# Down projection of an eight-core transformer layer: every second weight-tile load issued from GpSimd instead of SyncE

## What is computed

```python
def ternary_quant(w):
    scale = jnp.mean(jnp.abs(w)) + EPS
    q = jnp.clip(jnp.round(w / scale), -1.0, 1.0) * scale
    return w + jax.lax.stop_gradient(q - w)
...
x = x + attention(layernorm(x))             # [2048, 2048] on each core
h = layernorm(x)
up   = einsum('bsd,ed->bse', h, wu)         # 8192 expert columns
gate = einsum('bsd,ed->bse', h, wg)
hidden = silu(up) * gate
return x + einsum('bse,de->bsd', hidden, wd)    # the down projection
```

## Time and profile before

| What | Value |
|---|---|
| five runs, us | 8733.61, 9023.23, 9047.79, 9153.85, 9173.29 (median 9047.79) |
| the profiled execution, us | 8739.01 |
| its span on the slowest core (core 2), us | 8737.3 |
| spans of the eight cores, us | 8699.1 to 8737.3 |
| granted TensorE clock, mean over the span | 0.746 to 0.751 |
| PE busy | 4945.0 us, 57% of the span |
| down projection: first matmul to end of the span | 7272.3 to 8737.3 us |
| tile loads `td` from SP | 512, 128 KB each |

### The profile page before, as it was taken

One profiled execution on the slowest core, in us unless ns is written; L12 is line 12 of the kernel. 1 busy time (PEld: TensorE's weight loads), 2 busy tenths in 40 slices (PEclk: granted clock), 3 DMA queues, 4 the chain that ended last, 5 costly groups with the idle time before them and its releaser, 6 DMA issues.

```text
span 8737.3 us, 69328 instructions; the slowest of 8 cores (8699.1 to 8737.3 us)
## 1 busy us (share of the span) xinstructions
PE 4945.0 (57%) x22987; PEld 2188.1 (25%) x22987; DVE 3214.0 (37%) x4854; ACT 1724.8 (20%) x3014; POOL 638.7 (7%) x1086
## 2 busy tenths in 40 slices
PE   1534444444444434366211199999999995666775
PEld 1111111111111111122111144444444442222222
DVE  4044424433433334221566555555555540000000
ACT  3133323323322323111111111211212110000000
POOL 0111111111111111000000000000000000000000
PEclk9755565556565665677555599999999998898998
DMA  2322222222222222422344322212112113223222
GB/s 80 33 78 84 80 50 80 80 68 62 73 73 65 72 68 86 93 82 73 106 130 132 124 81 76 81 74 82 75 75 80 75 54 124 77 85 117 70 69 78
DMA packets 316026, 709.36 MB, mean 81 GB/s; under 512 B 123584, under 2 KB 189152, under 8 KB 283552
## 3 DMA queue, kind: packets, MB, share of 16 engines
q0 software_dynamic: 157216, 350.46, 14.5%
q1 hardware_dynamic: 158464, 354.47, 12.3%
HBM read 607.32 MB, written 109.05 MB: 82 GB/s over the span
## 4 chain that ended last, share of the span: by engine, by line
PE 48%; DMA 18%; DVE 13%; ACT 9%; issue 7%; POOL 2%; another core or an unknown queue 1%; SPq 1%; DVEq 0%; ACTq 0%; POOLq 0%
PE up_ps L1222 11%; PE gt_ps L1236 10%; DMA td<-tdT_scr 7%; DMA tdT_scr<-tds 5%; PE a_ps L461 5%; PE po_a L1319 3%; PE pr_ps L863 3%; PE y_ps L736 3%; PE pt_ps L616 3%; PE po_b L1319 3%; DVE stt L654 2%; ACT slabA L1152 2%; PE a_ps L646 2%; DMA xm<-xmid_scr 2%; ACT tds L1068 2%
## 5 line engine op out<-in xcount | busy, mean ns | idle before, releaser
L1222 PE MATMUL up_ps<-slabB,slabA 128*128 128x512 bf16 x4096 | 979.8, 401 | 59.9 <-ACT slabA L1152 59.9
L1236 PE MATMUL gt_ps<-slabB,slabA 128*128 128x512 bf16 x4096 | 905.0, 379 | 0.0
L616 PE MATMUL pt_ps<-id_bf,b 128*128 128x128 bf16 x2176 | 292.4, 303 | 593.9 <-DVE stt L678 315.2
L646 PE MATMUL a_ps<-k_bf,q_bf 128*128 128x512 bf16 (+3 forms) x640 | 258.1, 521 | 627.0 <-ACT w L690 379.1
L461 PE MATMUL a_ps<-slabA,wcol_bf 128*128 128x512 bf16 x1536 | 399.3, 426 | 310.0 <-DMA wcol_bf<-Wq 162.3
L1222 PEld LDWEIGHTS up_ps<-slabB,slabA 128*128 128x128 bf16 x4096 | 414.8, 102 | 594.1 <-issue 170.0
L1236 PEld LDWEIGHTS gt_ps<-slabB,slabA 128*128 128x128 bf16 x4096 | 400.8, 98 | 483.3
L1356 DVE SCALAR_TENSOR_TENSOR ost<-po_a,scl,xm 128x512 f32<-128x512 f32 x32 | 23.3, 748 | 1349.0 <-PE po_b L1319 1070.7
L690 ACT ACTIVATE w<-a_ps,stt 128x1024 f32<-128x1024 f32 (+7 forms) x384 | 328.3, 858 | 927.2 <-DVE stt L678 682.7
L1062 PE MATMUL tp_ps<-id_bf,b 128*128 128x128 bf16 x1024 | 139.6, 303 | 633.7 <-DMA tdT_scr<-tds 499.7
L1319 PE MATMUL po_a<-td,slabA 128*128 128x512 bf16 x1024 | 276.6, 394 | 379.6 <-DVE ost L1356 215.6
(11 more groups left out here) (168 smaller groups left out, 6300.6 us busy)
## 6 DMA issues: line engine op xcount, KB each, us to landing
pw<-W_down POOLq DMA_DIRECT2D x128, 512.0 KB, 4.3
pw<-W_up POOLq DMA_DIRECT2D x128, 512.0 KB, 4.3
pw<-W_gate POOLq DMA_DIRECT2D x128, 512.0 KB, 4.4
wd<-W_down SPq DMA_DIRECT2D x64, 1024.0 KB, 6.5
wu<-W_up SPq DMA_DIRECT2D x64, 1024.0 KB, 4.8
wg<-W_gate SPq DMA_DIRECT2D x64, 1024.0 KB, 6.9
td<-tdT_scr SPq DMA_DIRECT2D x512, 128.0 KB, 2.3
xt<-xb SPq DMA_DIRECT2D x32, 1024.0 KB, 6.3
```

What stands on the lines that cost most here:

```text
L616: e.transpose(pt_ps[:, par * 1024 + u * 128: par * 1024 + (u + 1) * 128], b1[:, jt * 128:(jt + 1) * 128], id_bf[:]), inc="t")
L646: e.matmul(a_ps[:, c * 512:c * 512 + n], q_bf[:, iq * 128:(iq + 1) * 128], k_bf[:, c * 512:c * 512 + n], start=True, stop=not last),
L1222: tc=tc, par=par: e.matmul(up_ps[:, sub * 512:(sub + 1) * 512], ttuA[par][:, dt * 128:(dt + 1) * 128], slabB[:, dt, tc * 512:(tc + 1) * 51 ...
L1236: par=par: e.matmul(gt_ps[:, tc * 512:(tc + 1) * 512], ttgA[par][:, dt * 128:(dt + 1) * 128], slabB[:, dt, tc * 512:(tc + 1) * 512], start ...
```

## The change

In the sweeps of the down projection the tiles of the even steps are still loaded by SP. The tiles of the odd steps are loaded by POOL, with POOL waiting for PE's `t`, and they count on the semaphore `ga` (used in an earlier stage for something else) instead of `u1`. Nothing else is changed: the same 512 transfers of 128 KB, two buffers, the same matmuls.

```diff
                         for et in range(64):
                             par = et % 2
                             td = (td0, td1)[par]
-                            tsm = ("u0", "u1")[par]
+                            tq = ("sync", "gpsimd")[par]
+                            tsm = ("u0", "ga")[par]
                             if et >= 2:
-                                ctx.wait("sync", "t", tb_par[par])
-                            ctx.dma("sync", td[:],
+                                ctx.wait(tq, "t", tb_par[par])
+                            ctx.dma(tq, td[:],
                                     tdT_dram[et * 128:(et + 1) * 128,
                                              dq * 512:(dq + 1) * 512], sem=tsm)
                             ctx.wait("tensor", tsm)
```

## The result

The changed kernel is slower: against the kernel before its time has the ratio 1.0235, 95% interval 1.0205 to 1.0264. Six runs gave a median of 9204.84 us (8935.74 to 9303.5); ten runs of before gave 9035.51 (8733.14 to 9173.29). The profiled execution took 8947.38 us, 208 us more than the one of before.

The account below looks back on a forecast made before the run. Each tile buffer's round trip, not PE, was taken to set the pace of the down projection. Pairs +130, fourth sweep +21 and between sweeps +3 gave +154 on 8739: 8893 us, range 8790 to 9010.

Parts of the forecast that it names:

- the odd buffer's round trip: Main term, in the down projection's sweeps: 4.36 us grows to 4.96, net +0.54 us a pair, +130 us on 241 pairs.
- POOL's time from issue to landing: Part of the odd buffer's round trip: POOL's odd tiles land 0.1 us later than SP's, ends -0.2 and +0.5.
- The reaction: Part of the odd buffer's round trip: POOL issues 0.50 us later than SP after the same matmul.
- Half of the 0.12 goes: Saving per pair of steps: even tiles have 0.6 us to spare, covering their share of 0.12 us of late landings.
- even with nothing between them, take 3.8: Matmul time of two steps in a sweep, 3.8 us, set against a buffer's round trip of 4.36 us.
- The fourth sweep: Term for odd tiles queued behind seven 2 MB loads on POOL: about +3 us each, +21 us, ends 0 and 32.
- the place behind the loads: In the fourth sweep, tile 9 behind a 2 MB load lands about 0.8 us later, with step 9 still to do.
- Between the sweeps: A sweep's first odd tile, queued behind the drain's last store, is 0.4 us late: +3 us for seven sweeps.
- The later landing: Rival: POOL's odd tiles land at the upper end, 2.8 us, adding 96 us: 8989 us; chance 0.17.
- The clock: Rival: PE's longer idle piece lowers its clock in one pair in four, +90 us: 8983 us; chance 0.10.
- The slack: Rival: odd tiles have slack, so only the fourth sweep and the boundaries cost: 8763 us; chance 0.07.
- the gain: Rival: two queues land sooner; POOL's landing at 1.6 us gains 0.26 a pair: 8700 us; chance 0.06.

Follow-up runs that it names:

- Experiment 5: Changed kernel with all tiles loaded by SP, which learns of a finished odd step through VectorE, first copying 256 numbers; ratio 1.0063 to the kernel before.
- experiment 3: Changed kernel with the eight 2 MB loads of the fourth sweep issued from ScalarE, odd tiles still from POOL; 8921.62 us.
- experiment 1: Changed kernel with odd tiles from ScalarE instead of POOL, a sweep's first odd tile waiting for the drain; spans of four undisturbed cores 8710.9 to 8730.1 us.
- experiment 2: Changed kernel with the odd tiles of the fourth sweep loaded by SP again; 8887.93 us.

## Why the prediction was wrong in size

The direction and the mechanism were right: the odd buffer's round trip sets the pace, even tiles have time to spare, and the fourth sweep pays again. The size was not: I gave 8893 us, +154 on the profiled execution, a ratio of 1.018, and +208 was measured in its like, a ratio of 1.0235. I gave "within 2%" 0.55 and "slower" 0.42, and it was slower. The range of 8790 to 9010 holds the profiled 8947.38, but not the median of the six runs, 9204.84. I built it on one execution, although the median of before lay 3.5% above that one already; a range meant for the median had to stand on the median. Of the signs that I named, POOL's issue 0.5 to 0.6 us after the step and waits in front of odd steps alone came true; the landing of 2.6 us lies above the 2.3 to 2.5, and a sweep takes 169.5 us and not 162, the fourth 242 and not 229.

- *The step that failed: POOL's time from issue to landing, "I take +0.1".* Measured: 2.6 us against 2.3, so +0.3. I had the bounds right (-0.2 and +0.5) and chose the wrong row to stand near. The line between POOL's own loads of 32 and 512 KB gave 2.8. What drew me down were POOL's stores (2.1 us), which go the other way, and the pair at 512 KB, where POOL and SP looked alike; but of that pair POOL loads one tile of 128 x 1024 float32 and SP gathers 128 x 2048 bf16 in blocks, so that equal times there did not mean equal times for one and the same tile. The estimate from the page "DMA: Bandwidth & Descriptors" of the Trainium skill, section Specifications, 0.4 later, which I kept out of the sum, was nearer than my choice: these runs show 0.3. On 241 pairs 0.2 us are 48 us. The time was 54 us over the forecast, and since the stage began 8 us earlier, this stage was 62 over: 49 in the seven sweeps, 13 in the fourth.
- *The reaction.* Forecast 0.50 later, measured 0.53 less 0.07 or 0.08: 0.46. Experiment 5 shows that such a delay alone is paid nearly in full.
- *"Half of the 0.12 goes", the late landings that even tiles no longer pass on.* Experiment 5 fits this saving (0.40 less 0.34 is 0.06 a pair), but does not show it: core for core the cost goes from 0.31 to 0.41. In the changed kernel it would be eaten up by late issues of POOL that I had not foreseen (last section). Put together for a sweep: 31 x (0.46 - 0.06) = 12.4 for the reaction, 31 x 0.3 = 9.3 for the landing, some 1.5 for the late issues and 0.6 for the late first odd tile are 23.8, where 23.7 were measured.
- *Two steps "even with nothing between them, take 3.8".* They take 3.61: in the pair above the even step starts 1.72 us after the odd one and ends at 7498.30. So PE's wait is 1.5 us and not the 1.0 to 1.3 forecast. The time of a pair goes by the round trip and did not hang on this.
- *The fourth sweep.* Forecast 13 for the pace and 21 for the place behind the loads; measured about 20 for the place, and 17 to 25 for all else (experiment 3). The reason given for the place holds. Before, PE stopped in front of the third step after a load (step 10 after the first load) and started it 9.3 us after the load's issue, the median of seven loads on six cores. Now it stops in front of the second (step 9) and starts it 9.8 us after: 0.5 later, forecast 0.8, with a step still to be done. That makes 7 x (0.5 + 1.89) = 17 us; with a split good to some 8 us, how near 21 came to 20 is luck. Of the 4 to 12 us by which the rest was short, 24 pairs at the same 0.2 us are 5; more was not taken apart.
- *Between the sweeps*, +3 forecast, with 0 and 8 as ends. The late first odd tile is there, 5.3 us of PE's waits on core 4. The 3.5 us by which the drains and the end are longer are another thing, and chance: in the mean of the six cores they are no longer than before (260.9 us against 261.5).
- *The rivals.* The later landing, to which I gave 0.17, is what happened, about half way to its 2.8. The clock was not at work in the ordinary sweeps: the granted clock is 0.97 to 0.99 in seven of them, as it was. The slack and the gain fell: PE waits for nearly every odd tile, POOL's landing is 2.6 us and not 1.6, and experiment 1 shows that a second engine alone changes nothing.

## What to carry to other kernels

When a double-buffered load is late, first add up the round trip of one buffer: the step itself, the reaction of the issuing engine, issue to landing, and the consumer's start. If that is longer than the steps which the buffers cover, a delay on the slower buffer is paid nearly in full at each turn, a second queue didn't help here, and more buffers did: four took seven of the eight sweeps from 146 to 113 us, with SP alone and with POOL. And a prefetch that is written behind a waiting transfer on the same engine is no prefetch: with POOL's 2 MB loads in its way, four buffers stopped PE as long as two did (8.85 us and 8.97 us).

## What the runs showed of the hardware that I had not expected

POOL now and then reacts late. In the second sweep of the changed kernel, step 17 ends at 7505.92 + 1.03 = 7506.95, and POOL issues the tile for step 19 at 7509.10, 2.15 us later instead of 0.54:

```profile
7505.92 1.03 PE L1320 MATMUL po_b<-td,slabA 128*128 128x512 bf16 x4
...
7509.10 0.54 POOL L62 DMA_DIRECT2D td<-tdT_scr  x1 [6.33 <-PE po_b L1320]
...
7512.10 1.02 PE L1320 MATMUL po_a<-td,slabA 128*128 128x512 bf16 x4 [3.42 <-DMA td<-tdT_scr]
...
7514.49 1.91 PE L1320 MATMUL po_a<-td,slabA 128*128 128x512 bf16 x4
```

PE waits 3.42 us instead of 1.5, and matmuls after it run at the lower clock for a while (four take 1.91 us instead of 1.03), together about 3.6 us. On all six cores with complete records this comes at the same steps (step 19 of the second sweep, 29 of the fifth, 51 of the seventh). In experiment 2 the second of the three comes at step 15 of the fifth sweep instead, and in experiment 3, with the 2 MB loads gone from POOL, only the first is left. So it goes with what POOL has issued by then and not with chance. No tile of SP or ScalarE is issued so late, before or in experiment 1; but POOL does it in the kernel before too, with the load behind step 31 of the fourth sweep, which ends at 7894.63 + 0.59 = 7895.22:

```profile
7894.63 0.59 PE L1319 MATMUL po_b<-td,slabA 128*128 128x512 bf16 x2
...
7897.37 0.88 POOL L62 DMA_DIRECT2D slabA<-hid_scr  x1 [25.23 <-issue]
```

That is 2.15 us again, so the sign of it could be seen ahead of the change. What POOL does in that time stays open.

And the two queues cut the same tile differently. The DMA queues of the page, before and then with the change:

```profile
q0 software_dynamic: 157216, 350.46, 14.5%
q1 hardware_dynamic: 158464, 354.47, 12.3%
```

```profile
q0 software_dynamic: 169504, 384.03, 15.3%
q1 hardware_dynamic: 121600, 320.90, 10.5%
```

256 tiles moved from one to the other. SP's queue lost 36864 packets, 144 for each tile; POOL's gained 12288, 48 for each. Fewer and larger packets did not land sooner; whether they are a part of the 0.3 us was not tried. Of that 0.3, 0.22 is as much as POOL's issue instruction is longer (0.54 against 0.32 us), which a run that varies the one without the other would have to show.
